# A scan kernel on one core: small steps moved between sections, and the last batch's drive rows scaled on ScalarE and turned back on TensorE

## The chip, the core and the metric

The kernel runs on one core of a Trainium2 chip. Its time is the device time of one execution in microseconds (us). A core has TensorE (PE; its weight loads are shown as PEld), VectorE (DVE), ScalarE (ACT), GpSimd (POOL) and SyncE (SP), which here only issues transfers. Each engine takes its instructions strictly in program order and waits on semaphores.

## What is computed

The input x has 4 batches of 1024 rows of 1024, the context 4 x 1024 x 512. A selective state space layer reads the context, is gated by the layer norm of x, and is added to x; then comes a dense layer with low-rank experts, top 2 of 8, added again.

```python
# per batch; e: 1024 channels, n: 16 states, t: 1024 steps
x_ = in_proj_w @ ctx.T;  u = silu(conv4(x_) + conv_b)
dt_lo, Bm, Cm = split(x_proj_w @ u)            # 32, 16, 16 rows
delta = softplus(dt_proj_w @ dt_lo + dt_proj_b)
def step(state, t):                            # state: e x n
    state = state * exp(delta_t * A) + (delta_t * u_t) * B_t
    y_t = sum_n(state * C_t)
y = (y + D * u) * silu(layernorm(x))
x = x + y
h = layernorm(x)
x = x + h @ W_base.T + b_base + sum over the top 2 experts of gate * (h @ A.T) @ B
```

All arithmetic is fp32, but for a few rows that are split into three bf16 parts before they are spread over the partitions.

## The kernel before

Work goes by 32 blocks, called E: batch b = E // 8, and channels r = E % 8 of 128 each. A block has 16 sections m = 0 to 15, one for each state n. Every engine has its own program, written out in `section(E, m)`, so the order of the work on each engine is fixed by hand. Times and steps below are named by block, section and scan.

One step n of a block is: a decay exp(delta * a_n) of 128x1024 by ScalarE (`make_decay`, L980); a drive du * B_n; the scan state = decay * state + drive by VectorE (`scan`, L1277); the product state * C_n by GpSimd (`product`, L1419), for which C_n is loaded as a row repeated over 128 partitions (`load_c`, c_rows); and eight 128x128 transposes by TensorE that add the product up in y_ps (`add_up`, `turn_into_y`, L586). `gated_y` (L1284) multiplies y_ps by the gate in section 2 of the next block. States and products have three buffers each, decays four, the PSUM pair row two.

The drive comes in one of three ways. ON_POOL rows are made by GpSimd from a repeated B row (`drive`, L1412), and their decay goes to row[n % 2], after scan n - 2. D rows are spread by TensorE (`spread`, L543) and multiplied by VectorE (L1259). ON_PE rows (K steps) are made by TensorE alone: `times_b` (L580) multiplies du transposed (`turn_du`, `take_du`) by a diagonal matrix of B_n, made once per batch by ScalarE (`make_diagonal`, L951), and VectorE needs no drive. Batch 0 has K rows 3, 5, 8, 10, 13, and the last batch, blocks 24 to 31, has 4, 8, 13; GpSimd drives 1, 6, 11, 14 in both. In the middle batches GpSimd drives 1, 3, 6, 11, 14 and in most blocks 8.

Beside the scans each block prepares the next: bias and softplus of delta (`take_v` L863, `soften` L870), gate (`gate_sum`, `gate_squares`, `gate_scale`, `gate_rows`, `turn_gate` L519, `take_gate` L856), du (GpSimd, `make_du`), and up to three halves of the next batch's projection and convolution (`project`, `begin_conv`, `taps`). gate_at and sizes_at give TensorE's sections for the gate turns and the bias matmuls, and ScalarE copies each result one section later; both use the one bank bank_b. The last block of a batch (7, 15, 23) also splits the next batch's B and C rows into bf16 parts: `split_first`, `split_second`, `split_third` on ScalarE, and between them `split_rest_of` twice on GpSimd.

From block 9 on, one row tile j = E - 9 of the dense layer runs beside each block: turn (L619), route (L626), `largest`, `first_gate` and `gates` on VectorE, `turn_gates` (L648) and `take_gates` (L1044, gT), `product` (L642) for two output halves, `experts` (L653), and `add_residual` (L1324) for each half. The second half's product waits for the first half's residual, as both use bank_a. Nine further tiles run alone as a tail after the last scan.

## Time and profile before

| | us |
|---|---|
| median of 3 runs | 2019.85 (2019.84 to 2026.95) |
| the profiled execution | 2023.09 |
| its span, first to last instruction | 2021.3 |
| TensorE busy | 1808.8 (89%) |
| VectorE busy | 1744.8 (86%) |
| GpSimd busy | 1681.3 (83%) |
| ScalarE busy | 1290.0 (64%) |
| block 0's first scan begins | 88.4 |
| the last scan ends | 1846.8 |

A busy TensorE is not TensorE at its peak: matmuls are pipelined and their ends modelled. A row of a timeline gives the start, the duration, the engine, the line, what is written and read, and in brackets how long the engine had been idle and who ended that. An engine's records may overlap by some 0.1 us, so that the distance of two starts is the better price of a repeated step.

### The profile page before, as it was taken

How to read it: one execution, taken by the hardware profiler on the slowest of the kernel's cores; microseconds unless marked ns; L12 is line 12 of the kernel's file. 1: busy time of each engine (PE TensorE's matmuls, PEld its weight loads, DVE VectorE, ACT ScalarE, POOL GpSimd, SP SyncE). 2: the span in 40 equal slices, each digit the busy share in tenths (PEclk: the TensorE clock that was granted, in tenths of full speed). 3: DMA queues.
4: the chain of work that ended last, by engine and by line, in shares of the span. 5: the costliest groups of instructions: out<-in, count | busy, mean ns of one | idle time of the engine just before them, and what ended most of it. 6: DMA issues, size and time to landing. Idle time of an engine off the chain costs nothing.

```text
span 2021.3 us, 25834 instructions
## 1 busy us (share of the span) xinstructions
PE 1808.8 (89%) x9000; PEld 1171.5 (58%) x9000; DVE 1744.8 (86%) x1397; ACT 1290.0 (64%) x1800; POOL 1681.3 (83%) x751
## 2 busy tenths in 40 slices
PE   8778888888788889899988899898999999989999
PEld 3346666666455555555555555565666666665554
DVE  3699999988999999999999999999999999995111
ACT  3485666666666676766676766666877777773332
POOL 0298999999998999999999999999999999997100
PEclk9889999998889999899999999999999999999999
DMA  4656666687786667697766676686676767666100
GB/s 160 213 199 211 218 209 205 211 298 268 240 283 215 217 201 223 219 311 256 250 221 218 205 230 212 213 299 224 233 226 225 227 227 224 226 228 246 57 31 32
DMA packets 158705, 435.01 MB, mean 215 GB/s; under 512 B 14608, under 2 KB 47632, under 8 KB 158576
## 3 DMA queue, kind: packets, MB, share of 16 engines
q1 hardware_dynamic: 155120, 420.79, 61.4%
q0 software_dynamic: 3456, 12.58, 3.2%
q8 instruction: 71, 1.16, 0.2%
q14 instruction: 58, 0.48, 0.1%
HBM read 382.46 MB, written 50.86 MB: 214 GB/s over the span
## 4 chain that ended last, share of the span: by engine, by line
DVE 38%; PE 31%; issue 15%; POOL 8%; ACT 6%; DMA 1%; DVEq 0%; POOLq 0%; SPq 0%; ACTq 0%
DVE state L1277 24%; DVE row L1259 9%; PE bank_a L642 6%; PE y_ps L586 6%; POOL prod L1419 5%; DVE conv L1251 3%; PE bank_b L642 3%; PE row L664 3%; POOL drive_rows L1412 2%; ACT decay L980 2%; PE row L580 2%; PE row L543 1%; PE bank_b L519 1%; PE bank_b L500 1%; ACT row L980 1%
## 5 line engine op out<-in xcount | busy, mean ns | idle before, releaser
L1419 POOL TENSOR_TENSOR prod<-state,c_rows 128x1024 f32<-128x1024 f32 x512 | 1209.5, 2393 | 101.1 <-PE y_ps L586 50.1
L1277 DVE TENSOR_TENSOR_SCAN state<-decay,row 128x1024 f32<-128x1024 f32 x355 | 808.8, 2283 | 21.0 <-PE row L580 13.5
L586 PEld LDWEIGHTS y_ps<-ident,prod 128*128 128x128 f32 x4096 | 488.0, 146 | 245.8 <-issue 158.7
L586 PE MATMUL y_ps<-ident,prod 128*128 128x128 f32 x4096 | 552.0, 282 | 46.2 <-POOL prod L1419 46.1
L642 PE MATMUL bank_a<-w_o,xnT 128*128 128x512 f32 x816 | 388.1, 606 | 12.3 <-DVE x L1324 12.3
L980 ACT ACTIVATE decay<-delta,a 128x1024 f32<-128x1024 f32 x355 | 397.3, 1137 | 1.5 <-DMA u_d<-decay 1.4
L1412 POOL TENSOR_TENSOR drive_rows<-du,b_rows 128x1024 f32<-128x1024 f32 x157 | 376.5, 2398 | 6.9 <-DMA b_rows<-bc_d 6.9
L1259 DVE TENSOR_TENSOR row<-du,row 128x1024 f32<-128x1024 f32 x296 | 358.1, 1210 | 25.1 <-PE row L543 24.8
L1277 DVE TENSOR_TENSOR_SCAN state<-row,drive_rows 128x1024 f32<-128x1024 f32 x157 | 357.3, 2276 | 19.3 <-POOL drive_rows L1412 15.5
L980 ACT ACTIVATE row<-delta,a 128x1024 f32<-128x1024 f32 x157 | 175.4, 1117 | 261.3 <-DVE state L1277 260.8
L543 PE MATMUL row<-parts,sel 96*128 96x512 bf16 x592 | 189.6, 403 | 80.7 <-DVE state L1277 74.3
L642 PEld LDWEIGHTS bank_a<-w_o,xnT 128*128 128x128 f32 x816 | 152.8, 194 | 154.7 <-issue 126.2
L1402 POOL TENSOR_TENSOR du<-delta,skip 128x1024 f32<-128x1024 f32 x32 | 75.9, 2371 | 80.4 <-ACT delta L874 80.4
L500 PE MATMUL bank_b<-ctx,w_in 128*128 128x512 f32 x288 | 131.3, 592 | 0.0
L816 ACT ACT_TABLE_LOAD x97 | 124.5, 1283 | 2.4 <-PEq L1503 0.7
L543 PEld LDWEIGHTS row<-parts,sel 96*128 96x128 bf16 x592 | 53.2, 102 | 112.2 <-DVE state L1277 97.5
L500 PEld LDWEIGHTS bank_b<-ctx,w_in 128*128 128x128 f32 x288 | 53.4, 190 | 53.5 <-issue 49.9
L1251 DVE SCALAR_TENSOR_TENSOR conv<-bank_b,ch,conv 128x512 f32<-128x512 f32 (+3 forms) x108 | 80.8, 748 | 3.2
L519 PE MATMUL bank_b<-ident,xrow 128*128 128x128 f32 x256 | 47.5, 315 | 39.7 <-ACT delta L863 26.0
L509 PE MATMUL bank_b<-xd,w_bdt 32*128 32x512 f32 x124 | 76.1, 696 | 3.5 <-ACT delta L863 3.5
L863 ACT ACTIVATE delta<-bank_b,ch 128x512 f32<-128x512 f32 x62 | 42.0, 678 | 56.6 <-PE bank_b L509 56.6
L580 PE MATMUL row<-w_o 128*128 128x128 f32 x560 | 73.5, 288 | 1.3 <-DVE state L1277 1.3
(160 smaller groups left out, 1879.3 us busy)
## 6 DMA issues: line engine op xcount, KB each, us to landing
c_rows<-bc_d SPq DMA_DIRECT2D x512, 512.0 KB, 4.6
xrow<-in_x SPq DMA_DIRECT2D x32, 512.0 KB, 5.3
skip<-u_d SPq DMA_DIRECT2D x32, 512.0 KB, 8.8
yy_d<-yy SPq DMA_DIRECT2D x32, 512.0 KB, 6.5
u_d<-conv SPq DMA_DIRECT2D x24, 512.0 KB, 5.3
ctx<-u_d SPq DMA_DIRECT2D x48, 256.0 KB, 6.2
x<-in_x SPq DMA_DIRECT2D x24, 512.0 KB, 5.8
x<-yy_d POOLq DMA_DIRECT2D x24, 512.0 KB, 9.5
```

Source lines behind the costliest of these rows:

```text
L500: last = nc.tensor.matmul(bank[:, :], w_in[:, U % 2, k, :], ctx[:, k, half(h)], start=(k == 0), stop=(k == NK - 1))
L543: last = nc.tensor.matmul(row[n % 2][:, half(h)], sel[:, SPREAD.index(n), :], parts[:, E // NE % 2, half(h)], start=True, stop=True)
L580: last = nc.tensor.matmul(row[n % 2][:, at], duT(E)[:, at], diagonal(b, n)[:, at], start=True, stop=True)
L586: last = nc.tensor.matmul(y_ps[:, i * P:(i + 1) * P], source[:, i * P:(i + 1) * P], ident[:, :], start=(first and i % (H // P) == 0), stop ...
L642: nc.tensor.matmul(at.sums[h][:, :], at.xnT[:, k, :], w_o[:, k, half(h)], start=(k == 0), stop=False)
L816: nc.scalar.preload_act_table_set(name)
L980: nc.scalar.activation(to[:, :], delta[:, E % 2, :], ACT.Exp, scale=a[:, E % NE, n:n + 1]).then_inc(decay_ready, 1)
L1251: nc.vector.scalar_tensor_tensor(to, bank[:, 0:end - h * H - back], ch[:, c, NC - 1 - back:NC - back], to, ALU.mult, ALU.add).then_inc(con ...
L1259: nc.vector.tensor_tensor(row[n % 2][:, :], du[:, E % 2, :], row[n % 2][:, :], ALU.mult).then_inc(dve_drive, 1)
L1277: nc.vector.tensor_tensor_scan(state[:, q % STATES, :], factor, term, 0.0, ALU.mult, ALU.add).then_inc(scan_done, 1)
L1412: nc.gpsimd.tensor_tensor(drive_rows[:, i % DRIVES, :], du[:, E % 2, :], b_rows[:, k, :], ALU.mult).then_inc(pool_drive, 1)
L1419: nc.gpsimd.tensor_tensor(prod[:, q % PRODS, :], state[:, q % STATES, :], c_rows[:, q % RING, :], ALU.mult).then_inc(prod_ready, 1)
```

## The change

Sections moved, in all dense blocks (9 on): TensorE's `turn_gates` goes from the start of section 11 to the end of section 10 and ScalarE's `take_gates` from after the silu of section 11 to ahead of the softplus of section 10. The second half's product is spread over sections 12 to 15 in place of 13 to 15 (in blocks with three projection halves it begins with 13, as before, but with three, two and three of the eight steps). VectorE adds the first half's residual in section 12, after drive 12, in place of 13. At the batch ends (7, 15, 23) ScalarE's second split goes from section 7 to 9, the third from 10 to 13, and GpSimd's second from 8 to 10.

The last batch: K rows become 4, 8, 11, 13 (row 11 was GpSimd's). No diagonals are made for it. Instead ScalarE scales the transposed du by B_n, which lies along the partitions there, in two half steps of four 128x128 activations (`scale_du`, sections in SCALED), and TensorE transposes the result back into row[n % 2]. w_in and w_x, no longer read by then, serve as the two buffers.

```diff
@@ -28,9 +28,6 @@
-DIAGONALS_AT = {(NBLK - NE - 1, 12): (B - 1, 4), (NBLK - NE, 2): (B - 1, 8), (NBLK - NE, 6): (B - 1, 13)}
-
-
 DECAY_AT = [(n - 2) % DS for n in range(DS)]
 DECAY_AT[12] = DECAY_AT[13] = 10
...
@@ -86,9 +83,13 @@
-DIAGONALS = {0: (3, 5, 8, 10, 13), B - 1: (4, 8, 13)}
-ON_PE = [DIAGONALS.get(E // NE, ()) if E else () for E in range(NBLK)]
-POOL_ROWS = {0: (1, 6, 11, 14), B - 1: (1, 6, 11, 14)}
+DIAGONALS = {0: (3, 5, 8, 10, 13)}
+
+SCALED = {4: (1, 2), 8: (4, 5), 11: (6, 7), 13: (8, 9)}
+TURNED = dict(DIAGONALS)
+TURNED[B - 1] = tuple(SCALED)
+ON_PE = [TURNED.get(E // NE, ()) if E else () for E in range(NBLK)]
+POOL_ROWS = {0: (1, 6, 11, 14), B - 1: (1, 6, 14)}
 ON_POOL = [(1, 6, 14) if E == NE - 1 else POOL_ROWS[E // NE] if ON_PE[E] else tuple(n for n in B_ROWS if n != 8 or len(HALVES[E]) > 1) for E in range(NBLK)]
 P_STEPS = [(E, n) for E in range(NBLK) for n in ON_POOL[E]]
 K_STEPS = [(E, n) for E in range(NBLK) for n in ON_PE[E]]
...
@@ -257,9 +258,10 @@
         def diagonal(b, n):
-            if b == 0:
-                return w_o[:, DIAGONALS[0].index(n), :]
-            return (b_rows[:, 1, :], b_rows[:, 3, :], conv[:, 0, :])[DIAGONALS[b].index(n)]
+            return w_o[:, DIAGONALS[b].index(n), :]
+
+        def scaled(i):
+            return (w_in[:, :, :, :].rearrange("p i k c -> p (i k c)"), w_x[:, :, :].rearrange("p k c -> p (k c)"))[i % 2]
         def duT(E):
             return w_o[:, len(DIAGONALS[0]), :] if E < NE else conv[:, 1, :]
...
@@ -572,12 +574,18 @@
             def times_b(E, n):
                 b, q = E // NE, E * DS + n
-                pe.wait_ge(diagonal_ready, diagonals_before(b, n))
-                pe.wait_ge(duT_ready, 2 * T_BEFORE[E] + 2)
+                if b in DIAGONALS:
+                    pe.wait_ge(diagonal_ready, DIAGONALS[b].index(n) + 1)
+                    pe.wait_ge(duT_ready, 2 * T_BEFORE[E] + 2)
+                else:
+                    pe.wait_ge(scaled_ready, scaled_index(E, n) + 1)
                 pe.wait_ge(scan_done, q - 1)
                 for c in range(NE):
                     at = slice(c * P, (c + 1) * P)
-                    last = nc.tensor.matmul(row[n % 2][:, at], duT(E)[:, at], diagonal(b, n)[:, at], start=True, stop=True)
+                    if b in DIAGONALS:
+                        last = nc.tensor.matmul(row[n % 2][:, at], duT(E)[:, at], diagonal(b, n)[:, at], start=True, stop=True)
+                    else:
+                        last = nc.tensor.transpose(row[n % 2][:, at], scaled(scaled_index(E, n))[:, at], ident[:, :])
                 last.then_inc(b_ready, 1)
             def turn_into_y(source, first, last_one):
...
@@ -758,15 +766,14 @@
                         k = 2 * at.index(m)
                         product(j, 0, [k, k + 1], beside, True)
                     if m == 11:
-                        turn_gates(j, beside, True)
-                    if m == 12:
                         experts(j, 0, beside)
                 for i, at in enumerate(front_plan(E)[0]):
                     if m in at and len(HALVES[E]) > i and m >= 9:
                         project(E, i, [k for k in range(NK) if at[k % len(at)] == m])
                 if dense:
-                    if m >= 13:
-                        product(j, 1, range(2 * (m - 13), NE if m == 15 else 2 * (m - 13) + 2), beside, True)
+                    if m >= 12:
+                        ks = ((), (0, 1, 2), (3, 4), (5, 6, 7)) if len(HALVES[E]) > 2 else ((0, 1), (2, 3), (4, 5), (6, 7))
+                        product(j, 1, ks[m - 12], beside, True)
                     if m == 15:
                         experts(j, 1, beside)
@@ -776,6 +783,8 @@
                     add_up(q - 2)
                 if m == 6:
                     add_skip(E)
+                if dense and m == 10:
+                    turn_gates(j, beside, True)
                 if m == 15 and E + 1 < NBLK and ON_PE[E + 1]:
                     turn_du(E + 1, 0)
@@ -944,13 +953,27 @@
             def make_diagonal(b, n, cs):
                 act.wait_ge(bT_ready, 1 if b == 0 else 2)
-                if b and 0 in cs:
-                    act.wait_ge(u_out[0], 16 * NBLK // 2)
-                    act.wait_ge(pool_drive, P_BEFORE[b * NE])
                 for c in cs:
                     last = nc.scalar.activation(diagonal(b, n)[:, c * P:(c + 1) * P], ident[:, :], ACT.Copy, scale=bT[:, c, n:n + 1])
                 if NE - 1 in cs:
                     last.then_inc(diagonal_ready, 1)
+
+            def scale_du(E, n, h):
+
+                i = scaled_index(E, n)
+                if h == 0:
+                    act.wait_ge(bT_ready, 2)
+                    act.wait_ge(duT_ready, 2 * T_BEFORE[E] + 2)
+                    if i >= 2:
+                        act.wait_ge(b_ready, R_INDEX[K_STEPS[K_INDEX[E, n] - 2]] + 1)
+                    else:
+                        act.wait_ge(x_ready, len(HALF_INDEX))
+                        act.wait_ge(us_used, (B - 1) * 2 * NE)
+                for c in range(h * NE // 2, (h + 1) * NE // 2):
+                    at = slice(c * P, (c + 1) * P)
+                    last = nc.scalar.activation(scaled(i)[:, at], duT(E)[:, at], ACT.Copy, scale=bT[:, c, n:n + 1])
+                if h:
+                    last.then_inc(scaled_ready, 1)
             def take_du(E, h):
@@ -1121,6 +1144,10 @@
                     take_du(E, 0)
                 if m == (0 if E < NE else 1) and ON_PE[E]:
                     take_du(E, 1)
+                if b == B - 1:
+                    for n, at in SCALED.items():
+                        if m in at:
+                            scale_du(E, n, at.index(m))
                 if dense and m == 7:
                     exp_gap(j)
                 last = r == NE - 1 and b + 1 < B
...
@@ -1139,7 +1166,7 @@
                     take_gate(E, gate_at(E).index(m - 1))
                 if last and m - 1 in sizes_at(E):
                     take_v(E + 1, sizes_at(E).index(m - 1))
-                if last and m == 7:
+                if last and m == 9:
                     split_second(b + 1)
                 if dense and m == 5:
                     take_routing(j, beside)
@@ -1152,8 +1179,10 @@
                         gate_scale(E + 1)
                 if r == NE - 2 and b + 1 < B and m == 9:
                     take_xd(b + 1, 0)
-                if last and m == 10:
+                if last and m == 13:
                     split_third(b + 1)
+                if dense and m == 10:
+                    take_gates(j, beside)
                 if E + 1 < NBLK:
                     if m == 10:
@@ -1162,10 +1191,6 @@
                     if m == 11:
                         table(SILU)
                         gate_rows(E + 1)
-                if dense and m == 11:
-                    take_gates(j, beside)
-                if (E, m) in DIAGONALS_AT:
-                    make_diagonal(*DIAGONALS_AT[E, m], range(NE))
                 if E == 0 and m >= FIRST_PIECE:
                     for k in PIECES[m - FIRST_PIECE]:
                         make_diagonal(0, DIAGONALS[0][k // 4], range(2 * (k % 4), 2 * (k % 4) + 2))
@@ -1367,7 +1392,7 @@
                     else:
                         dve.wait_ge(gate_copied, 2 * E + 2)
                     gates(j, beside)
-                if dense and m == 13:
+                if dense and m == 12:
                     add_residual(j, 0, beside)
                 scan(E, m)
                 if m == 2 and E:
...
@@ -1454,7 +1479,7 @@
                 product(E * DS + m)
                 if j >= -1 and m == 6:
                     add_yy(j + 1, E if r == 0 else E - 1)
-                if r == NE - 1 and b + 1 < B and m in (6, 8):
+                if r == NE - 1 and b + 1 < B and m in (6, 10):
                     split_rest_of(b + 1, m == 6)
                 if m == 12 and E + 1 < NBLK:
                     make_du(E + 1)
```

## Rows read from the trace of the kernel before

**Rows 1.** Windows, blocks 20, 28: us, busy PE PEld DVE ACT POOL, clock, DMA, GB/s
```profile
1206.10:1265.60 59.50, 54.59 (x257) 34.48 (x256) 57.42 (x49) 39.23 (x55) 54.47 (x25) 0.94 0.67 208
...
1642.10:1693.10 51.00, 47.98 (x284) 33.93 (x283) 49.49 (x37) 37.09 (x52) 49.63 (x23) 1.00 0.74 227
```

**Rows 2.** Timeline of VectorE in block 28: scans 1 and 8, drive 12, residual
```profile
1645.65 2.29 DVE L1277 TENSOR_TENSOR_SCAN state<-row,drive_rows 128x1024 f32<-128x1024 f32 x1 [0.70 <-POOL drive_rows L1412]
...
1668.15 2.29 DVE L1277 TENSOR_TENSOR_SCAN state<-decay,row 128x1024 f32<-128x1024 f32 x1 [0.35 <-PE row L580]
...
1680.01 1.21 DVE L1259 TENSOR_TENSOR row<-du,row 128x1024 f32<-128x1024 f32 x1
...
1683.45 0.69 DVE L1324 TENSOR_TENSOR x<-x,bank_a 128x512 f32<-128x512 f32 x1
```

**Rows 3.** Costliest groups by line, kept apart by form: GpSimd's drive; count, busy, mean ns
```profile
L1412 POOL TENSOR_TENSOR drive_rows<-du,b_rows 128x1024 f32<-128x1024 f32 x157 | 376.5, 2398 | 6.9 <-DMA b_rows<-bc_d 6.9
```

**Rows 4.** Timeline of TensorE in block 28
```profile
1660.90 0.65 PE L519 MATMUL bank_b<-ident,xrow 128*128 128x128 f32 x4 [0.47 <-ACT gate L856]
...
1666.16 1.95 PE L580 MATMUL row<-b_rows,conv 128*128 128x128 f32 x16
1667.95 1.04 PE L586 MATMUL y_ps<-ident,prod 128*128 128x128 f32 x8
1668.82 0.60 PE L543 MATMUL row<-parts,sel 96*128 96x512 bf16 x2
...
1680.24 2.02 PE L580 MATMUL row<-conv 128*128 128x128 f32 x16 [0.68 <-DVE state L1277]
1682.29 1.13 PE L653 MATMUL bank_a<-w_bdt,gT 65*128 65x512 f32 x2
```

**Rows 5.** Timeline of ScalarE: block 23 (two rows), block 28 (three)
```profile
1409.17 2.12 ACT L928 ACTIVATE parts<-xd 32x1024 bf16<-32x1024 f32 x2 [6.52 <-POOL xd L1444]
...
1428.28 2.45 ACT L951 ACTIVATE b_rows<-ident,bT 128x128 f32<-128x128 f32 x8 [0.74 <-POOL drive_rows L1412]
...
1658.17 1.12 ACT L980 ACTIVATE row<-delta,a 128x1024 f32<-128x1024 f32 x1 [2.34 <-DVE state L1277]
...
1660.28 0.57 ACT L856 ACTIVATE gate<-bank_b 128x512 f32<-128x512 f32 x1
...
1668.53 1.06 ACT L823 ACTIVATE xrow<-xrow 128x1024 f32<-128x1024 f32 x1 [4.49 <-DMA xrow<-in_x]
```

**Rows 6.** Timeline of TensorE and VectorE in blocks 21 and 22
```profile
1312.88 3.78 PE L642 MATMUL bank_a<-w_o,xnT 128*128 128x512 f32 x4 [2.81 <-DVE x L1324]
...
1319.08 1.23 DVE L1259 TENSOR_TENSOR row<-du,row 128x1024 f32<-128x1024 f32 x1 [1.88 <-PE row L543]
...
1366.55 2.07 PE L653 MATMUL bank_a<-w_bdt,gT 65*128 65x512 f32 x2 [1.53 <-ACT gT L1044]
```

**Rows 7.** Windows after the wait in block 21, and around the like in block 18
```profile
1311.90:1318.70 6.80, 5.82 (x14) 3.32 (x15) 5.30 (x4) 6.64 (x12) 6.80 (x4) 0.50 0.55 165
...
1131.00:1141.20 10.20, 5.82 (x28) 3.47 (x29) 10.17 (x7) 9.32 (x12) 9.14 (x4) 1.00 0.49 174
```

**Rows 8.** Timeline of GpSimd and VectorE in block 23
```profile
1394.52 2.35 POOL L1419 TENSOR_TENSOR prod<-state,c_rows 128x1024 f32<-128x1024 f32 x1 [1.94 <-PE y_ps L586]
...
1416.89 1.23 DVE L1259 TENSOR_TENSOR row<-du,row 128x1024 f32<-128x1024 f32 x1 [3.50 <-PE row L543]
...
1421.17 4.68 POOL L1419 TENSOR_TENSOR prod<-state,c_rows 128x1024 f32<-128x1024 f32 x2 [0.73 <-DVE state L1277]
```

**Rows 9.** Timeline of GpSimd: block 7, block 15
```profile
501.38 2.36 POOL L1419 TENSOR_TENSOR prod<-state,c_rows 128x1024 f32<-128x1024 f32 x1 [1.49 <-DMA c_rows<-bc_d]
...
962.24 2.34 POOL L1419 TENSOR_TENSOR prod<-state,c_rows 128x1024 f32<-128x1024 f32 x1 [2.22 <-DMA c_rows<-bc_d]
```

**Rows 10.** Timeline of VectorE and TensorE in block 20, section 12
```profile
1249.07 1.21 DVE L1259 TENSOR_TENSOR row<-du,row 128x1024 f32<-128x1024 f32 x1
...
1249.65 1.02 PE L653 MATMUL bank_a<-w_bdt,gT 65*128 65x512 f32 x2
```

18 lines of the change are left out of this document (9 added, 9 removed).

## The prediction

> **What bounds the kernel now.** The page's shares come first: four engines are between 64% and 89% busy, so no total decides. Next I read the windows of single blocks (a block is one E, 16 scans). A middle block takes 59.5 us, of which VectorE works 57.4 and GpSimd 54.5; a block of the last batch takes 51.0, of which GpSimd works 49.6, VectorE 49.5, TensorE 48.0 and ScalarE only 37.1 [rows 1]. Two engines are full in the last batch. VectorE's timeline of block 28 then shows what it still waits for: 0.70 us at scan 1 for GpSimd's drive row, 0.35 at scan 8 for TensorE's diagonal step, nothing elsewhere [rows 2]. Its own chain is the floor of such a block, 51.05 - 0.70 - 0.35 = 50.0 us, so about one microsecond per block is all that can be had there. Last I read TensorE and ScalarE in that block, since both get new work ahead of someone who waits.
>
> **Part 1, the last batch (blocks 24 to 31).** Row 11 leaves GpSimd, a drive of 2.4 us per block [rows 3]. GpSimd falls to some 47.3 us, and the drive of row 1, queued behind the products of rows 13 and 14, comes in time. The 0.70 us goes in blocks 25 to 31 (in 24 GpSimd starts level): -4.9 us. Late next is what TensorE and ScalarE do, below.
>
> TensorE: a diagonal step is 16 matmul records, from 1666.16 to 1667.95, 1.79 us; 8 transposes take 0.87 (1667.95 to 1668.82) [rows 4], and I price the new ones by that. Three steps of 1.79 become four of 0.87, 1.9 us less work. By itself that gains nothing: TensorE was last only at scan 8.
>
> ScalarE: eight activations of 128x128 took 2.45 us, 0.31 each [rows 5]; 32 per block are 9.8 us, a half step (four) 1.2. 37.1 + 9.8 = 46.9 of 50 fits in sum. In place, the two halves for row 4 and the first for row 8 fall into ScalarE's waits of sections 1 to 4, those for 11 and 13 into the 4.49 us for which it stood for xrow [rows 5]. The second half for row 8 is the exception. It is issued in section 5, behind the exponential of row 6, which waits for scan 4 (2.34 us), and ahead of the copy of gate half 0 at 1660.28 [rows 5]. TensorE's turn of gate half 1 needs the same bank and waits for just that copy, 0.47 us now [rows 4]. The copy comes 1.2 us later and TensorE arrives 0.9 earlier (row 4's step is shorter): a wait of 0.47 + 1.2 + 0.9 = 2.6 us. Queued behind it is everything up to the step of row 8, which begins 1666.16 - 1660.90 = 5.26 us after the turn. That step ends 1.2 later for its start and 0.9 earlier for its length, so 0.3 later against scan 4, and scan 8 waits 0.6 in place of 0.35: 0.25 x 8 = +2 us.
>
> The residual: VectorE now adds it in section 12, after drive 12. The expert matmul that it needs stands in TensorE's section 12 behind the step of row 13, which waits for scan 11. Scan 11 ended at 1680.01 and the step began 0.23 later [rows 2, 4]. New, after scan 11: 0.2 + 0.9 (transposes) + 1.0 (experts, from their 1.13 on record less overlap) + 0.1 = 2.2 us; VectorE has done its drive after 1.2. It waits 1.0 us, with scan 12 and all later scans behind it, where in section 13 it went straight on from 1683.45 [rows 2]. 1.0 x 8 = +8 us.
>
> At an unchanged clock the last batch costs -4.9 + 2 + 8 = +5.1 us.
>
> **The clock.** In the last batch TensorE's granted clock is 1.00 (2.4 GHz) [rows 1]. In block 21 TensorE waited 2.81 us for the residual, four product records then took 3.78 us, and VectorE waited 1.88 us for a spread; in block 22 it waited 1.53 us for gT, and two expert records took 2.07 in place of 1.02 [rows 6]. In the 6.8 us that followed block 21's wait the grant was 0.50 (1.2 GHz); in block 18, with a like wait, it was 1.00 throughout [rows 7]. A wait of 2.6 us may therefore bring the fall or not; two waits of three did, and I take 6 blocks of 8. The loss for the step of row 8 lies between 0 and half of those 6.8 us, 3.4; I take the middle, 1.6, since part of such a stretch lies in the wait or behind the step: 6 x 1.6 = +9.6.
>
> A rule of the Trainium skill speaks against the new transposes. TensorE: Matmul & The Clock Gate, Part 4: PE-mode transpose, says that a transpose does not count as busy for the clock gate in the way of a matmul. In block 28 so far the trace does not agree: 160 of TensorE's 284 records are transposes (17 x 8 for y, 24 others), and the grant stayed at 1.00 [rows 1]. Rival D is what the rule would do.
>
> **Part 2, blocks 7 to 23.** At the end of batch 2 ScalarE stood 6.52 us for GpSimd's first split [rows 5], with the bias copy of the next block behind it; TensorE, and with it the spread of row 10, came late, and VectorE waited 3.50 us [rows 8]. The split in section 9 frees that copy. But GpSimd binds here, with 24 long instructions: of its own waits, 1.94 and 0.73 us [rows 8] can go, and VectorE can run ahead by some 1.7 more (three state buffers) into block 24, where GpSimd is then lighter: -4.3 us. The three diagonals leave ScalarE, which helps only VectorE here. In block 15 nothing comes of it: GpSimd waits 2.22 us for c_rows, a transfer issued long before. In block 7 the second split used to lie ahead of such a wait (1.49 us) [rows 9] and now comes after it: +0.7.
>
> Gates turned a section earlier: the 1.53 us of block 22 [rows 6] passes from TensorE to ScalarE, ahead of softplus, silu and the exponential of row 14; that has more than this before scan 14, so nothing, up to 1.5 in a block if it hadn't. With the product spread over four sections TensorE is 0.9 to 1.7 us lighter at a block's end. That frees blocks 11, 13, 14, 21 and 22: the 1.88 [rows 6] in 13 and 21, and waits of below 1 us at starts; net of the new residual wait I take -1.3, -2.0 and -2.0.
>
> The residual costs here as well: in block 20 the experts end 1.02 us after 1249.65, at 1250.67, and VectorE is free at 1249.07 + 1.21 = 1250.28 [rows 10]: 0.4 to 0.5 us. In the nine blocks where VectorE binds (9 to 12, 16 to 20) 9 x 0.45 = +4.1.
>
> Middle: -4.3 + 0.7 - 1.3 - 2.0 - 2.0 + 4.1 = -4.8 us.
>
> **Sum.** 5.1 + 9.6 - 4.8 = +9.9; I take +9, as the last block also hands over to the tail from a lighter GpSimd. The profiled execution took 2023.09 us (span 2021.3 and 1.8 around it), 3.2 over the median of 2019.85: 2032.1 on its scale, 2028.8 on the median's.
>
> **Rivals.**
> A, the forecast (0.43): waits traded, and the clock falls in most blocks of the last batch; 2023 to 2036.
> B (0.25): the waits as priced, the clock holds. 5.1 - 4.8 = +0.3: 2020. For it is block 18, against it 21 and 22.
> C, faster (0.13): TensorE, 1.9 us lighter, is early enough that neither scan 8 nor the residual waits. The last batch sits on its floor, 7 x -1.05 - 0.35 = -7.7; with -4.8, 2007.4. It decides where the experts end less than 1.2 us after scan 11; row 13's wait for scan 11 speaks against it.
> D, slower (0.12): transposes don't hold the clock up, it falls in every block and for as long as in block 21. 8 x 3.4 over B: +27.5, 2047; 2062 if the residual's chain (1.9 us more) is hit too.
> E, slower (0.07): ScalarE becomes the bound. From section 5 on, five new half steps, 6.0 us, meet a wait of 4.5; 1.5 us per block over B is +12, 2032. It decides if ScalarE has no second slack behind section 8. The Trainium skill's ScalarE: Activation LUTs, Rules for kernel authors, gives 0.3 us and 0.83 ns per element, by which I estimate 0.41 us for one of these and 13 us per block, over ScalarE's room; the trace's 0.31 speaks against it.
>
> 0.5%, 10.1 us, is about what a measurement can tell from no change. Of A, 0.26 lies below +10.1 and 0.17 above. Same: 0.26 + 0.25 = 0.51; slower: 0.17 + 0.12 + 0.07 = 0.36; faster: 0.13. The range leaves out most of C and of D: 2010 to 2042; A's own is 2023 to 2036.
>
> **What would show it.** In a block of the last batch: no wait for drive_rows at scan 1; 1.0 us for the experts at the residual; TensorE 2.6 us for the gate copy, and then 0.6 us (clock held) or some 2.2 (fallen) at scan 8; a granted clock below 1.00; a length of 51.6 or 53.2 us. In block 23: no wait for the spread of row 10. In block 20: 0.5 us at the residual. I am wrong if the clock stays at 1.00 in the last batch, if the experts are done before drive 12, or if GpSimd is still last at scan 1.

## The result and the profile after

The changed kernel takes 2037.14 us (median of 14 runs, 2030.21 to 2047.98); the kernel before, run between them, 2021.52 us (14 runs, 2019.13 to 2028.24). The ratio is 1.0071, 95% interval [1.0058, 1.0085]: slower by 0.7%. The profiled execution took 2035.78 us, its span 2034.0, that is 12.7 us more than the 2021.3 of before.

A block's length is read from one scan 0 to the next on VectorE. From before to after:

| stretch | before | after | difference |
|---|---|---|---|
| up to the first scan | 88.4 | 86.7 | -1.7 |
| blocks 0 to 6 | 370.1 | 369.0 | -1.1 |
| blocks 7, 8 | 112.8 | 113.1 | +0.3 |
| blocks 9 to 22 | 808.4 | 809.1 | +0.7 |
| block 23 | 59.1 | 53.8 | -5.2 |
| blocks 24 to 31 | 408.1 | 427.7 | +19.6 |
| tail | 174.4 | 174.6 | +0.2 |

In these two profiles the loss lies in the last batch, and there in blocks 24 to 28: 55.94, 55.23, 54.47, 54.62 and 54.78 us. Blocks 29 to 31 take 50.91, 51.33 and 50.45, about as long as before (51.05, 51.03, 51.63). Windows of after (us, busy time of PE, PEld, DVE, ACT, POOL, granted clock, DMA, GB/s): block 23, block 28, block 29, and a stretch of 13.7 us inside block 28.

```profile
1377.80:1431.60 53.80, 49.78 (x252) 30.33 (x250) 51.76 (x39) 40.99 (x56) 53.80 (x26) 1.00 0.70 232
...
1651.90:1706.70 54.80, 51.56 (x270) 35.84 (x269) 49.50 (x38) 46.48 (x84) 47.58 (x22) 0.88 0.65 211
1706.70:1757.60 50.90, 45.77 (x267) 31.52 (x265) 49.49 (x38) 45.99 (x84) 46.98 (x22) 1.00 0.67 226
...
1656.90:1670.60 13.70, 13.17 (x44) 8.94 (x45) 10.60 (x7) 10.08 (x20) 8.10 (x5) 0.51 0.75 237
```

VectorE works 49.5 us in both blocks, ScalarE 46 where it was 37.09, GpSimd 47 where it was 49.63 [rows 1]. What parts block 28 from block 29 is the granted clock: each of blocks 24 to 28 has one stretch of 13.7 us at 1.2 GHz (1.00 is 2.4 GHz), and TensorE is busy for 13.17 us of it. Before, the clock was 1.00 in the whole batch.

TensorE of after at the start of block 28 (start, length, line, operation; in brackets the idle time before it and who ended it):

```profile
1652.43 0.60 PE L570 MATMUL bank_b<-ident,du 128*128 128x128 f32 x4
...
1655.25 0.66 PE L570 MATMUL bank_b<-ident,du 128*128 128x128 f32 x4 [1.34 <-ACT conv L985]
...
1657.43 1.97 PE L594 MATMUL y_ps<-ident,prod 128*128 128x128 f32 x8 [1.09 <-POOL prod L1444]
...
1663.09 1.91 PE L588 MATMUL row<-ident,w_in 128*128 128x128 f32 x8
...
1670.86 0.60 PE L545 MATMUL row<-parts,sel 96*128 96x512 bf16 x2
```

It waits 1.34 us for ScalarE's copy of du and 1.09 for a product. Inside the second wait, at 1656.8, the clock falls, and the eight matmuls behind it take 1.97 us, where they took 1.09 before. The same place before, TensorE and then ScalarE:

```profile
1644.49 0.60 PE L568 MATMUL bank_b<-ident,du 128*128 128x128 f32 x4
...
1645.80 0.64 PE L568 MATMUL bank_b<-ident,du 128*128 128x128 f32 x4
...
1648.00 1.09 PE L586 MATMUL y_ps<-ident,prod 128*128 128x128 f32 x8 [1.13 <-POOL prod L1419]
...
1645.12 0.60 ACT L962 ACTIVATE conv<-bank_b 128x512 f32<-128x512 f32 x1 [0.93 <-PE bank_b L568]
```

and ScalarE after:

```profile
1654.62 0.57 ACT L985 ACTIVATE conv<-bank_b 128x512 f32<-128x512 f32 x1
```

Counted from scan 0 (1642.1 before, 1651.9 after), ScalarE's copy stands at +3.0 and +2.7 us, so ScalarE is not late. TensorE is early: its first turn of du stands at +2.4 before and at +0.5 after, since its product ended earlier. What it gained it spends waiting: 2.43 us in two waits, where it was 1.13 in one.

VectorE of after, block 28 and block 29:

```profile
1655.09 2.29 DVE L1302 TENSOR_TENSOR_SCAN state<-row,drive_rows 128x1024 f32<-128x1024 f32 x1 [0.33 <-POOL drive_rows L1437]
...
1671.50 1.23 DVE L1284 TENSOR_TENSOR row<-du,row 128x1024 f32<-128x1024 f32 x1 [3.93 <-PE row L545]
...
1694.13 0.68 DVE L1349 TENSOR_TENSOR x<-x,bank_a 128x512 f32<-128x512 f32 x1
...
1709.72 2.29 DVE L1302 TENSOR_TENSOR_SCAN state<-row,drive_rows 128x1024 f32<-128x1024 f32 x1 [0.18 <-POOL drive_rows L1437]
...
1726.24 0.16 DVE L1316 MAX8 top<-hl 128x8 f32<-128x8 f32 x1 [0.58 <-issue]
```

Its 3.93 us at drive 5 are where the fall is paid: the spread of row 5 (1670.86 above) is the first work behind the stretch at half clock, and late by what stood ahead of it there. The residual at 1694.13 waits for nothing, and scan 1 still waits for GpSimd's drive row. New is 0.58 us ahead of the search for the largest (MAX8), whose releaser the trace doesn't name.

### The profile page after: what moved, and what is told of

Same layout as the page of the kernel before. It is cut to its first block, busy times and chain, and to the rows that moved or that the text cites. A ratio compares the mean times of both kernels' runs of the same rounds, so it can differ in the third digit from the quotient of the medians.

```text
span 2034.0 us, 25831 instructions
## 1 busy us (share of the span) xinstructions
PE 1818.6 (89%) x8872; PEld 1177.8 (58%) x8872; DVE 1743.7 (86%) x1397; ACT 1358.4 (67%) x2032; POOL 1663.7 (82%) x743
## 4 chain that ended last, share of the span: by engine, by line
DVE 35%; PE 31%; issue 13%; POOL 10%; ACT 9%; DMA 2%; DVEq 0%; SPq 0%; POOLq 0%; ACTq 0%
DVE state L1302 22%; DVE row L1284 8%; PE y_ps L594 6%; POOL prod L1444 6%; PE bank_a L650 4%; DVE conv L1276 3%; PE bank_b L650 3%; PE row L672 2%; POOL drive_rows L1437 2%; ACT decay L1003 2%; PE bank_b L511 2%; PE bank_b L502 2%; PE bank_b L521 2%; ACT L825 2%; PE row L545 2%
## 5 line engine op out<-in xcount | busy, mean ns | idle before, releaser
L1302 DVE TENSOR_TENSOR_SCAN state<-decay,row 128x1024 f32<-128x1024 f32 x363 | 824.6, 2282 | 18.7 <-PE row L586 11.3
L594 PEld LDWEIGHTS y_ps<-ident,prod 128*128 128x128 f32 x4096 | 499.4, 148 | 265.2 <-issue 162.9
L594 PE MATMUL y_ps<-ident,prod 128*128 128x128 f32 x4096 | 563.3, 285 | 57.7 <-POOL prod L1444 57.5
L1003 ACT ACTIVATE decay<-delta,a 128x1024 f32<-128x1024 f32 x363 | 407.1, 1136 | 1.3 <-DVE state L1302 1.2
L1437 POOL TENSOR_TENSOR drive_rows<-du,b_rows 128x1024 f32<-128x1024 f32 x149 | 355.4, 2385 | 5.6 <-DMA b_rows<-bc_d 5.6
L1302 DVE TENSOR_TENSOR_SCAN state<-row,drive_rows 128x1024 f32<-128x1024 f32 x149 | 339.5, 2278 | 23.5 <-POOL drive_rows L1437 19.6
L1003 ACT ACTIVATE row<-delta,a 128x1024 f32<-128x1024 f32 x149 | 166.3, 1116 | 206.3 <-DVE state L1302 205.2
L521 PE MATMUL bank_b<-ident,xrow 128*128 128x128 f32 x256 | 51.5, 336 | 48.5 <-ACT delta L872 34.0
L511 PE MATMUL bank_b<-xd,w_bdt 32*128 32x512 f32 x124 | 84.7, 768 | 0.1
L502 PEld LDWEIGHTS bank_b<-ctx,w_in 128*128 128x128 f32 x288 | 53.4, 190 | 51.2 <-issue 46.5
L521 PEld LDWEIGHTS bank_b<-ident,xrow 128*128 128x128 f32 x256 | 35.6, 169 | 71.6 <-ACT delta L872 41.9
L832 ACT ACTIVATE xrow<-xrow 128x1024 f32<-128x1024 f32 x32 | 33.7, 1053 | 64.6 <-DMA xrow<-in_x 64.6
```

The costliest lines, as they stand in the source:

```text
L502: last = nc.tensor.matmul(bank[:, :], w_in[:, U % 2, k, :], ctx[:, k, half(h)], start=(k == 0), stop=(k == NK - 1))
L521: last = nc.tensor.transpose(bank_b[:, c * P:(c + 1) * P], xrow[:, h * H + c * P:h * H + (c + 1) * P], ident[:, :])
L594: last = nc.tensor.matmul(y_ps[:, i * P:(i + 1) * P], source[:, i * P:(i + 1) * P], ident[:, :], start=(first and i % (H // P) == 0), stop ...
L1003: nc.scalar.activation(to[:, :], delta[:, E % 2, :], ACT.Exp, scale=a[:, E % NE, n:n + 1]).then_inc(decay_ready, 1)
L1302: nc.vector.tensor_tensor_scan(state[:, q % STATES, :], factor, term, 0.0, ALU.mult, ALU.add).then_inc(scan_done, 1)
L1437: nc.gpsimd.tensor_tensor(drive_rows[:, i % DRIVES, :], du[:, E % 2, :], b_rows[:, k, :], ALU.mult).then_inc(pool_drive, 1)
```

## The experiments

Two theories. W: TensorE, made lighter by both parts, runs ahead, waits longer for ScalarE or GpSimd, the clock falls behind such a wait, and VectorE loses what the half clock costs. T: the transposes that took the place of matmuls don't hold the clock. The kernels were not all timed beside the same runs of before, so ratios are to be compared and not medians. Last batch and block 23 are from the one profiled execution; before: 408.1 and 59.1. Such an execution can lie off the median: that of product_late, 2023.06 us, is the fastest of its ten, that of filled_by_transposes, 2027.93, the second of nine, and that of filled_all, 2023.10, the slowest of ten.

| kernel | median (runs) | ratio [95%] | blocks 24 to 31 | block 23 |
|---|---|---|---|---|
| after | 2037.14 (14) | 1.0071 [1.0058, 1.0085] | 427.7 | 53.8 |
| moves_only | 2031.57 (6) | 1.0034 [1.0019, 1.0048] | 411.9 | 57.3 |
| scaled_only | 2042.72 (4) | 1.0087 [1.0064, 1.0109] | 423.1 | 59.3 |
| splits_only | 2022.59 (10) | 1.0000 [0.9986, 1.0014] | 407.8 | 58.3 |
| turned_by_matmul | 2035.75 (5) | 1.0062 [1.0041, 1.0083] | 423.5 | 53.8 |
| product_late | 2032.99 (10) | 1.0039 [1.0018, 1.0061] | 415.6 | 53.8 |
| filled_last | 2028.06 (10) | 1.0028 [1.0014, 1.0042] | 412.7 | 53.8 |
| filled_by_transposes | 2032.41 (9) | 1.0047 [1.0031, 1.0063] | 413.7 | 53.8 |
| filled_all | 2017.03 (10) | 0.9960 [0.9945, 0.9976] | 419.7 | 53.4 |
| moves_filled | 2011.05 (4) | 0.9933 [0.9917, 0.9950] | 408.3 | 56.9 |
| before_filled | 2021.62 (10) | 0.9984 [0.9969, 0.9999] | 409.8 | 58.0 |

**One part alone.** Before with part 2 only (sections and splits, the three diagonals kept), and with part 1 only (ScalarE's scaled drives).

> The kernel before with the second half of the change alone: gates, experts, product and first residual one section earlier, splits later; the last batch keeps its three diagonal rows and GpSimd's row 11. In the changed kernel block 23 shrank from 59.0 to 53.8 us, and blocks 9 to 22 kept their sum (808.4 to 809.1). Theory W (the clock falls because TensorE, lighter at the end of a block, waits at the start of the next): TensorE is lighter here too, by the 1.7 us of the product, but the diagonal steps keep 1.8 us each and GpSimd holds the pace, so the waits in sections 0 to 2 stay near 2 us; granted clock 1.00 or nearly so in the last batch, blocks of 51, total 2014 to 2019. Theory T (the transposes in place of matmuls let the clock fall): no such transposes here, clock 1.00, the same total. If the moves alone are what spoils the last batch, blocks of 54 to 55 and a total above 2030.

> The kernel before with the first half of the change alone: rows 4, 8, 11, 13 scaled by ScalarE and transposed back, everything else in its old section. Theory W: with the product still over three sections TensorE reaches the block's start late, the waits in sections 0 to 2 stay below 2 us, the clock holds, blocks of 50.5 to 51.5, total 2015 to 2022. Theory T: the transposes are all there, so the clock falls as in the changed kernel, blocks of 54 to 55 in most of the last batch, total 2033 to 2045.

Neither is a gain, and W's totals are missed in both. The moves cost 0.34%, where both theories had expected 2014 to 2019 us. In their profile blocks 24 and 26 to 31 take 50.8 to 51.6 us, block 25 has 6.8 us at half clock and takes 53.31, and blocks 9 to 22 take 812.8 us for 808.4: blocks 11, 14, 16 and 19, at full clock before, get 6.8 us of half clock each, as in after. At its blocks' starts TensorE of moves_only waits in one piece, 2.0 to 2.7 us, and only block 25 falls behind that. A wait of that length is thus not enough by itself:

```profile
1551.36 1.09 PE L586 MATMUL y_ps<-ident,prod 128*128 128x128 f32 x8 [2.66 <-POOL prod L1420]
```

This is block 26, where the clock stayed at 1.00. Part 1 alone costs 0.87%, against what W had expected and within T's 2033 to 2045 us: the clock falls with the old schedule of the product too, in six of the eight blocks. Its profile shows why. TensorE of scaled_only in sections 12 of blocks 25 and 29, and windows right after these waits:

```profile
1532.45 2.07 PE L661 MATMUL bank_a<-w_bdt,gT 65*128 65x512 f32 x2 [1.95 <-ACT gT L1066]
...
1742.68 1.13 PE L661 MATMUL bank_a<-w_bdt,gT 65*128 65x512 f32 x2 [2.50 <-ACT gT L1066]
...
1532.50:1539.30 6.80, 6.80 (x14) 3.63 (x15) 4.97 (x4) 6.76 (x9) 6.80 (x4) 0.50 0.43 151
...
1744.10:1747.50 3.40, 3.40 (x10) 1.84 (x9) 3.40 (x3) 3.37 (x6) 3.40 (x2) 0.50 0.22 51
```

Here ScalarE, with 46 us of work, is late with gT, TensorE waits 1.95 and 2.50 us for it, and the clock falls. Blocks 24, 26 and 30 fall behind the same wait (1.93, 1.72, 1.78), while 27 and 28 have it as well (1.73, 1.75) and hold. It is W's mechanism at another wait; my price for W had only the wait at the block's start in it. In after the gates are turned a section earlier, and this wait is at most 0.89 us, while those at the block's start have come.

**The splits alone** (before with the splits and ScalarE's part of them in the new sections):

```diff
-                if last and m == 7:
+                if last and m == 9:
                     split_second(b + 1)
-                if last and m == 10:
+                if last and m == 13:
                     split_third(b + 1)
-                if r == NE - 1 and b + 1 < B and m in (6, 8):
+                if r == NE - 1 and b + 1 < B and m in (6, 10):
```

> The kernel before with the three batch ends alone changed: second split in section 9, third in 13, GpSimd's second in 10. In the changed kernel block 23 took 53.8 us against 59.0, with the gates moved as well 57.3 once. Theory: the wait of 3.5 us for the spread of row 10 goes, block 23 takes 55 to 57, blocks 9 to 22 are those of before (808 us), the last batch stays at 51.0 per block, total 2 to 4 us below before. Rival: GpSimd binds in block 23 and nothing is gained, or the last batch's clock, undisturbed before, falls as its first block begins differently, total above before.

1.0000: no gain, where 2 to 4 us had been expected. Block 23 is 0.8 us shorter. The 3.50 us that VectorE waited there [rows 8] are gone, but it now waits 1.88 us for the experts at the residual of section 13 and 2.12 at scan 14. In moves_only the residual's wait is gone too, and scan 14 waits for its decay, which stands in ScalarE's queue behind the diagonal for row 4:

```profile
1433.71 2.29 DVE L1278 TENSOR_TENSOR_SCAN state<-row,drive_rows 128x1024 f32<-128x1024 f32 x1 [4.65 <-ACT row L981]
```

Only in after, without that diagonal, is this wait down to 1.04 us and the block to 53.8, with GpSimd busy in all 53.80 us of it (window above). Block 23's gain needs all three.

**The transposes.** After, with the step of the scaled drive as a matmul:

```diff
-                        last = nc.tensor.transpose(row[n % 2][:, at], scaled(scaled_index(E, n))[:, at], ident[:, :])
+                        last = nc.tensor.matmul(row[n % 2][:, at], scaled(scaled_index(E, n))[:, at], ident[:, :], start=True, stop=True)
```

> The changed kernel, but the scaled rows are turned by a plain fp32 matmul with the identity (16 records a step) and not by 8 transposes. Theory T: the clock holds or comes back after 3 to 7 us, blocks of about 51, total below 2025. Theory W: the waits that precede the fall lie ahead of row 4's step and remain, the clock falls in at least as many blocks, each step costs 1.8 us (3.6 at half clock) instead of 0.9 (1.9), total 2037 to 2050.

One step and block 28 of turned_by_matmul:

```profile
1658.42 2.02 PE L588 MATMUL row<-ident,w_in 128*128 128x128 f32 x16 [0.64 <-DVE state L1302]
...
1649.80:1702.20 52.40, 49.27 (x300) 35.56 (x299) 49.45 (x37) 46.05 (x84) 47.40 (x22) 1.00 0.70 220
```

The step is 16 records and 0.9 us longer. The clock falls in blocks 24 (6.8 us), 25 and 31 (3.4 us each), and holds in 26 to 30; but these now take 52.5 us, 1.2 more than with transposes at full clock. The time is that of after. Against W's expectation the waits at the start are shorter: 0.44 and 0.41 us in block 28 in place of 1.34 and 1.09, since the longer steps bring TensorE there later. So more work on TensorE holds the clock in most of the batch, and costs as much; T's total (below 2025) is missed as well. As this edit changes the waits and the transposes at once, it does not separate W from T.

**The product later in the last batch** (after, sections 13 to 15 in the last batch):

```diff
                         ks = ((), (0, 1, 2), (3, 4), (5, 6, 7)) if len(HALVES[E]) > 2 else ((0, 1), (2, 3), (4, 5), (6, 7))
+                        if b == B - 1:
+                            ks = ((), (0, 1), (2, 3), (4, 5, 6, 7))
```

> The changed kernel, but in the last batch the second half's product is again in sections 13 to 15 (two, two, four of the eight steps), all else as changed. Theory W: TensorE is 1.7 us later at the start of a block, its waits in sections 0 to 2 shrink from 2.4 to about 1 us, the clock stays at 1.00 in the last batch, blocks of 50.5 to 51.5 and a total of 2010 to 2018. Theory T: clock and blocks as in the changed kernel, 2033 to 2040.

TensorE at the start of block 28:

```profile
1643.33 0.66 PE L570 MATMUL bank_b<-ident,du 128*128 128x128 f32 x4 [0.28 <-ACT conv L987]
...
1645.73 1.09 PE L594 MATMUL y_ps<-ident,prod 128*128 128x128 f32 x8 [1.31 <-POOL prod L1446]
```

It comes later to the turn of du and waits 0.28 us in place of 1.34, and then 1.31 for the product in place of 1.09: 1.59 us in sum, where it was 2.43. Blocks 25 to 28 take 51.3 us, and after block 24 (10.2 us at half clock) there are only single falls of 3.4 us, in 28, 30 and 31. The last batch is 12.1 us shorter than in after, but this is the fastest of ten executions. The ratio is 1.0039 for 1.0071: by the medians the later product gives back about half the loss, and the total that W had expected (2010 to 2018) is missed by 15 us. So what the moved product freed on TensorE is one part of what brought the falls.

**The waits filled.** After, with matmuls of zeros on TensorE, added into y_ps ahead of its two waits at the block's start. It is extra work, 2.5 us per block of the last batch:

```diff
+            def fill_y(E, times):
+                pe.wait_ge(zero_set, 1)
+                for i in range(times):
+                    nc.tensor.matmul(y_ps[:, half(i % 2)], zero[:, :], parts[:, E // NE % 2, half(i % 2)],
+                                     start=False, stop=False, skip_group_check=True)
...
+                if m == 0 and E >= (B - 1) * NE:
+                    fill_y(E, 5)
                 if m == 0 and E >= NE and ON_PE[E]:
                     turn_du(E, 1)
...
+                if m == 1 and E >= (B - 1) * NE:
+                    fill_y(E, 5)
                 if q >= 2 and m != 2:
```

> The changed kernel with work that computes nothing put into TensorE's two waits at a block's start, in the last batch only: five bf16 matmuls of a matrix of zeros added to y_ps ahead of the second turn of du, and five ahead of the summing of the previous block's row 15, 0.2 us each. In the changed kernel TensorE waited 1.35 and 1.09 us there, the granted clock fell in blocks 24 to 28 for 13.7 us each and they took 54.5 to 55.9 us; blocks 29 and 30, with the clock at 1.00, took 50.9 and 51.3. If the waits bring the fall (theory W): clock 1.00 in nearly all of the last batch, its eight blocks 410 us in place of 428, total 2018 to 2026. If the transposes do (theory T), or if it is not the clock that costs: no change, 2033 to 2042, or a little more for the added work.

TensorE at the start of block 28 of filled_last, and the window of that block:

```profile
1651.97 1.24 PE L597 MATMUL y_ps<-parts,zero 96*128 96x512 bf16 x5
1653.22 0.66 PE L572 MATMUL bank_b<-ident,du 128*128 128x128 f32 x4
...
1655.69 1.09 PE L609 MATMUL y_ps<-ident,prod 128*128 128x128 f32 x8 [0.30 <-POOL prod L1464]
...
1649.90:1701.60 51.70, 48.30 (x282) 32.96 (x281) 49.49 (x38) 45.84 (x84) 47.80 (x22) 1.00 0.70 226
```

The clock is 1.00 in blocks 25 to 31, which take 50.4 to 51.7 us; the last batch is 15.0 us shorter than in after, by work that computes nothing. Of the +19.6 of after's profile 15 are therefore the clock; of the 4.6 left 3.9 stand in block 24, which here still falls for 3.4 us. By the ratios, 1.0071 and 1.0028, the fill gives back some 9 us, more than half of the loss. The 0.28% that stays is about what the moves cost alone (0.34%). The median is 2 us over what W had expected.

**The same fill by transposes**, to separate W and T:

```diff
-                    nc.tensor.matmul(y_ps[:, half(i % 2)], zero[:, :], parts[:, E // NE % 2, half(i % 2)],
-                                     start=False, stop=False, skip_group_check=True)
+                    nc.tensor.matmul(y_ps[:, i % NE * P:(i % NE + 1) * P], zero[:, :], ident[:, :],
+                                     start=False, stop=False, is_transpose=True, skip_group_check=True)
```

(ten for five, which take the same 1.25 us)

> As filled_last, but the two waits at the start of a block of the last batch are filled with ten transposes of a 128x128 fp32 matrix of zeros each, 0.11 us apiece, in place of five matmuls of 0.2. filled_last held the clock in blocks 25 to 31 and took 2028 us against 2037. If transposes hold the clock up like matmuls: the same, clock 1.00 in those blocks, 2024 to 2032. If they do not count (the Trainium skill, TensorE: Matmul & The Clock Gate, Part 4: PE-mode transpose): the clock falls as in the changed kernel, 2034 to 2042.

The whole last batch of its profile:

```profile
1434.90:1849.00 414.10, 385.15 (x2292) 272.61 (x2293) 394.98 (x295) 356.40 (x648) 378.60 (x169) 1.00 0.71 227
```

Blocks 25 to 28 take the same 51.3 us as in filled_last's blocks 25 to 27, at a clock of 1.00 (block 24 has one fall of 3.4 us, which the mean of the batch rounds away): transposes held it here, which speaks against T. Against T speaks filled_last too, as after's own transposes are all in it. But this profile is of the second fastest of nine executions. The median, 2032.41 us, lies between the two expectations, the ratio is 0.2% above filled_last's, and the intervals overlap, so whether transposes hold the clock as often in every execution stays open.

**Two steps of the prediction undone**, with one execution each. First the experts left in section 12, with the residual in 12 (this is the arrangement that the prediction had priced):

```diff
-                    if m == 11:
+                    if m == 12:
                         experts(j, 0, beside)
```

> The changed kernel, but TensorE's expert matmul of the first half stays in section 12, behind the step of row 13, while VectorE adds the residual in section 12: the arrangement that the prediction priced. By that price VectorE waits 1.0 us at the first residual in each block of the last batch (0.45 in block 20), 8 us and 4 us in sum. If the price is wrong, the wait is below 0.3.

2032.7 us. VectorE in block 28 of experts_12:

```profile
1691.82 0.69 DVE L1349 TENSOR_TENSOR x<-x,bank_a 128x512 f32<-128x512 f32 x1 [0.99 <-PE bank_a L661]
```

It is 0.98 to 0.99 us in every block of the last batch, and 0.44 in blocks 22 and 23: the waits of the prediction (1.0 and 0.45), which after doesn't have. But the block is not 1.0 us longer for it. At full clock, blocks 28 to 30 take 51.5 us, those of filled_last mostly 51.3: VectorE, held up at the residual, no longer waits 0.2 to 0.9 us for GpSimd's row at scan 1 nor 0.2 at scan 14. Second, each half step placed behind the gate's copy of its section in ScalarE's queue; the one meant is the second for row 8:

> The changed kernel, but ScalarE copies gate half 0 ahead of the half step for row 8 and not behind it. In the changed kernel TensorE waited 2.39 us for that copy in blocks 29 and 30, at full clock. By the prediction's working 1.2 us of that are the half step: here the wait is 1.2 us in blocks at full clock, and the blocks are no shorter than 50.5. If ScalarE is late for another reason, the wait stays above 2.

2041.06 us. TensorE in block 29, of after and then of gate_copy_first:

```profile
1726.14 0.66 PE L521 MATMUL bank_b<-ident,xrow 128*128 128x128 f32 x4 [2.39 <-ACT gate L865]
```
```profile
1726.26 0.66 PE L521 MATMUL bank_b<-ident,xrow 128*128 128x128 f32 x4 [1.19 <-ACT gate L865]
```

The wait goes from 2.39 to 1.19, by the 1.2 us of the half step, and block 29 takes 50.46 for 50.91. The clock still falls in blocks 24 to 28, where it falls in after, and in block 30 as well: not this wait but those of the block's start come ahead of these falls.

**The middle filled too.** filled_all is filled_last with more fill: eight matmuls into bank_a ahead of the gate's turn in section 2 (blocks 9 to 22 but 15), not of zeros but with a result that is overwritten unread, and matmuls of zeros, twelve (blocks 1 to 8) or six (9 to 23), ahead of the row spread of section 11; moves_filled is moves_only with all of this fill, before_filled is the kernel before with it.

> filled_last with TensorE's waits filled in the other blocks too, by matmuls that compute nothing: eight into bank_a ahead of the gate turn of section 2 (blocks 9 to 22, a wait of 2.0 to 2.9 us there), six into y_ps ahead of the spread of section 11 (twelve in blocks 1 to 8). In the runs so far a microsecond at half clock has cost about 0.25 us. The middle blocks had 6.8 us at half clock in most; if the clock holds there, blocks 9 to 22 come down from 812 to 800 to 805 and the total to 2012 to 2020, below the kernel before. If the added work is itself in the way, or the falls come from other waits, 2026 to 2034.

> moves_only (last batch with diagonals, as before) with all the same fill. It keeps the last batch's 408 to 412 us and should have the middle of filled_all: 2010 to 2018 if the clock is what costs there, 2026 to 2034 if not.

> The kernel before with the same matmuls of zeros as moves_filled (five before the second turn of du and five before the sum for row 15 in each block from 24 on, eight ahead of the first gate's turn in blocks 9 to 22 but 15, twelve or six ahead of the row spread in section 11), and nothing else; the output is unchanged. It tells how much of moves_filled's gain (0.9933) is the fill and how much the moves. If the fill alone makes it: 0.993, 2008 to 2012 us, and the moves are worth nothing. If the moves are needed for it (the gate copy and the product spread over four sections), blocks 9 to 22 stay above 803 us instead of 798.8, block 23 stays at 58 to 59 us instead of 56.9, and the ratio is 0.996 to 0.998. I expect the latter for block 23 alone and the former for blocks 9 to 22: 0.994 to 0.995.

Block 19, at full clock in both, of moves_filled and then of before_filled:

```profile
1147.10:1204.80 57.70, 55.33 (x271) 33.68 (x270) 57.00 (x49) 39.82 (x56) 56.24 (x26) 1.00 0.66 226
```
```profile
1152.10:1211.00 58.90, 57.21 (x276) 34.80 (x276) 57.38 (x49) 39.63 (x56) 55.55 (x25) 1.00 0.67 221
```

moves_filled beats both kernels: 2011.05 us, 0.9933. The fill alone gives 0.9984, the moves alone cost 0.34%, together they gain 0.67%. Where both are at full clock the moves save 1.2 us in each of blocks 11, 14, 19 and 22, 4.8 us in all; 0.6 to 1.7 they save in 10, 13, 18, 20, 21 and 15, where before_filled still fell; 12 and 17 are level, and 16 is 2.8 us longer, with a fall of its own. Blocks 9 to 22 take 798.8 us in moves_filled, 807.0 in before_filled, 808.4 before and 812.8 in moves_only (but see the last section on how far one profile carries for these blocks). I had expected most of that gain from the fill itself. In filled_all the last batch falls again, for 3.4 us in each of blocks 26 to 31, at 1657.9 in block 28, 1.4 us after the end of the gate's wait of 2.39 us; blocks 26 to 30 take 52.7 to 53.3 us instead of 51.3, block 31 51.2. In filled_last the last batch has the same instructions and the same wait of 2.39 us in every block, and only block 24 falls. So with part 1 in the kernel that wait may bring a fall or not; without part 1 it is 0.47 us (moves_filled), and the last batch has no fall.

## Why the prediction was right or wrong

The forecast was the right case, the clock falling in most blocks of the last batch, with the time 8 us too low (2028.8, measured 2037.1, inside 2010 to 2042 but just above that case's own 2023 to 2036); against the median of before beside it after lies 15.6 us over, where +9 was said. For the last batch at an unchanged clock +5.1 was said, and filled_last shows +4.6 (with one fall of 3.4 us in it); that this is so near is luck in part, for the +8 in it did not come and little of the -4.9 did. Two of the three signs of being wrong that the prediction names did come: the experts are done when VectorE asks for them, and GpSimd is still last at scan 1.

- **The residual, +8 and +4.1: wrong, a misreading of the change.** I left the experts in TensorE's section 12; the diff moves them to 11, behind the step of row 11 and ahead of that of row 13. After has no wait at the residual (1694.13 above). experts_12 shows that the wait was sized rightly, 0.98 and 0.44 us, and the place was not. These 12.1 us should have been 0. It also shows that in the last batch the waits at the residual and at scan 1 hang together: with the first the second goes, and the block, 51.6 us by my working, takes 51.5; without it 51.3. So the wait itself lengthens a block there by 0.2 us and not by 1.0. In the middle the price did hold in block 9, which has no fall in either kernel: 58.24 us for 57.71.
- **The clock, +9.6: mechanism right, place and size wrong.** I counted one fall in six of eight blocks, behind the wait for the gate's copy, at 1.6 us. That wait came, 2.39 for 2.6 predicted, but only in blocks 29 to 31, which held their clock behind it. The fall came behind the block's start in five blocks, lasted 13.7 us, and cost 3.2 to 3.9 us in each of blocks 25 to 28 (over 51.3); filled_last puts the whole at 15.0 us in the profiles and some 9 by the ratios. I had taken it that a lighter TensorE gains nothing, and didn't ask where TensorE would wait instead. In moving two product steps forward I had booked only their use, 0.9 to 1.7 us at the block's end. filled_last shows that the falls are most of the loss in the last batch, product_late that this lightness is one cause of them; moves_only, as light in the product and with longer single waits, falls in one block, so it takes part 1 as well, and in what way isn't shown. In filled_all six of eight blocks do fall for 3.4 us behind the gate's wait, at 1.4 to 2.0 us in five of them, as priced; so that danger was real, only not met in after's profile.
- **Scan 1, -4.9: wrong.** 1.68 us in block 24 and, but for block 26, 0.18 to 0.59 in the others are still there. GpSimd in block 29:

```profile
1720.16 2.35 POOL L1444 TENSOR_TENSOR prod<-state,c_rows 128x1024 f32<-128x1024 f32 x1 [1.20 <-DVE state L1302]
...
1738.34 2.37 POOL L1444 TENSOR_TENSOR prod<-state,c_rows 128x1024 f32<-128x1024 f32 x1 [0.97 <-DVE state L1302]
1742.37 4.68 POOL L1444 TENSOR_TENSOR prod<-state,c_rows 128x1024 f32<-128x1024 f32 x2 [1.66 <-DVE state L1302]
1747.01 2.36 POOL L1437 TENSOR_TENSOR drive_rows<-du,b_rows 128x1024 f32<-128x1024 f32 x1
1749.33 2.37 POOL L1444 TENSOR_TENSOR prod<-state,c_rows 128x1024 f32<-128x1024 f32 x1
1751.66 2.37 POOL L1427 TENSOR_TENSOR du<-delta,skip 128x1024 f32<-128x1024 f32 x1
1754.00 4.69 POOL L1444 TENSOR_TENSOR prod<-state,c_rows 128x1024 f32<-128x1024 f32 x2
```

  The 2.4 us saved lie ahead of section 12, and there GpSimd catches up with VectorE and waits (1.20, 0.97, 1.66). Behind the last wait its queue is as full as before up to the drive of row 1. I took a saving in the sum for a saving at the point where somebody waits. With VectorE 1.0 us later at the residual, as I had it, the wait does go (experts_12, blocks 26 and 28 to 31).
- **Scan 8, +2: not there**, but 0.58 us ahead of the search for the largest, which I hadn't priced. ScalarE's queue in block 29 shows what it is:

```profile
1724.34 1.26 ACT L974 ACTIVATE w_x<-conv,bT 128x128 f32<-128x128 f32 x4
1725.51 0.58 ACT L865 ACTIVATE gate<-bank_b 128x512 f32<-128x512 f32 x1
1725.98 0.21 ACT L1054 ACTIVATE hl<-bank_a 128x72 f32<-128x72 f32 x1
```

  The search reads hl, whose copy ends at 1726.19, 0.05 us before the search begins; the half step for row 8 stands ahead of that copy, too; I had followed only the gate's copy behind it. That the half step is the cause is read from this order; no run takes it from there (in gate_copy_first it is still ahead of that copy, and the wait is 0.59). Without falls a block of the last batch is mostly 51.3 us and not on its way to 50.0.
- **ScalarE and TensorE's new work: right.** Four activations take 1.2 us (0.3 each), ScalarE works 46.5 us in block 28 (46.9 said), eight transposes start 0.87 us before what follows them. The Trainium skill's ScalarE: Activation LUTs, Rules for kernel authors, is where my estimate of 0.41 us for each comes from. The trace agrees with it for one activation by itself, which lasts 0.39 us, but in a row they overlap and start 0.29 apart, and the queue pays only that.
- **Block 23, -4.3 with 24: right in kind.** The wait of 3.50 us is gone and the block is 5.2 us shorter, in good part because the diagonal is gone from ScalarE's queue (4.65 us of waiting at scan 14 in moves_only, 1.04 in after), but block 24 begins with GpSimd behind and gives 5.7 back, most of it in its fall: with the clock kept better the two take 107.9 (filled_last) and 105.8 us (filled_all) for 109.3 before.
- **Blocks 9 to 22, -1.2 in all: +0.7 in the profile**, of which the moved work saves some 8 us where the fill holds most of the clock (moves_filled against before_filled, with part of it falls that before_filled has), and falls take it back without the fill (moves_only).
- **Rivals.** B lost to the clock. C's condition, no wait at the residual, came true by the misreading, and its time did not: the other waits took its place. D's trigger, the rule that transposes don't hold the clock up, is not what the profile of filled_by_transposes shows: with them in the waits the grant was 1.00 in blocks 25 to 31. The Trainium skill's TensorE: Matmul & The Clock Gate, Part 4: PE-mode transpose, states that rule; this profile does not agree. D's price, 3.4 us a block, is about what four blocks lost all the same, by another cause. E, ScalarE as bound, is seen in part, as the late gT: 1.7 to 2.5 us in scaled_only, 0.66 to 0.89 in after's blocks 25 to 28.

Open: why a fall lasts 13.7 us in after, experts_12 and gate_copy_first, with TensorE busy almost throughout, and mostly 3.4 or 6.8 in the other kernels; and why it comes behind one wait of a given size and not behind the next (block 25 has 1.08 and 1.34 us at its start, block 30 has 1.09 and 1.34, and only 25 falls).

## What to carry to other kernels

Taking work off an engine is not free when another engine's chain sets the pace: ask at which wait the saved time reappears, for TensorE because its clock may fall behind it, for a queue like GpSimd's because relief ahead of its last wait never reaches who waits behind it. Price an edit with the clock held (matmuls of zeros in the waits), and then without; here the moves gain 0.5% with the fill, which holds most of the clock, and lose 0.3% without. A wait that is priced rightly need not lengthen the block by as much: look which other wait it takes away. And read the diff for every line that moves, context lines under a changed condition too.

## What the runs showed of the hardware

- The granted clock fell for 3.4, 6.8, 10.2 or 13.7 us at a time. 13.7 us at 1.2 GHz cost 3.2 to 3.9 us of a block in which TensorE has 46 of 51 us of work.
- Five short matmuls of zeros (1.24 us) in each of two waits of about that length came with 2.4 GHz in seven blocks of eight in the profile of filled_last; ten fp32 transposes of zeros in each did the same in theirs. In filled_all, with the same matmuls there, six blocks fell behind another wait.
- TensorE waited 2.66 us (moves_only, block 26) and 2.39 us (after, blocks 29 to 31), and the clock did not fall behind that.
- Between executions, equal instructions give unequal falls: blocks 9 to 22 are the same code in after and filled_last, and took 809.1 and 818.7 us in their profiles; before and splits_only took 808.4 and 817.1 there, and the last batch of filled_last and filled_all 412.7 and 419.7. The loss of one profile is therefore not the loss of the median, and a few us between two profiles of different kernels show nothing by themselves.
